# Moving the head sums, the attention product and the weight splits in a fused attention and mixture-of-experts kernel

## The chip, the cores and the metric

One core of one Trainium2 chip runs the kernel. The metric is the device time of one execution in microseconds, as the median of several runs.

## The reference

With `x` of 1 x 1024 x 256 (float32) and `xn` its layernorm, the output is `x + attention(xn) + ffn(xn)`:

```python
qkv = xn @ w_qkv                                  # 256 x 768; 16 heads of 16
q, k = elu(q) + 1, elu(k) + 1
decay = sigmoid(decay_param)                      # one per head
s_t  = decay * s_{t-1} + k_t * v_t                # running_kv
z_t  = decay * z_{t-1} + k_t                      # running_ksum
den  = clip(sum_over_head(q * z), 1e-6)
attention = (q * s / den) @ w_out

e    = argmax(xn @ router_w.T)                    # 8 experts, top 1
gate = sigmoid(top logit)
routed = (silu(g) * u) @ w_down[e],  g, u = split((xn * gate) @ w_gate_up[e])
shared = (silu(g) * u) @ shared_down, g, u = split(xn @ shared_gate_up)
ffn  = routed + shared                            # inner width 512
```

## The kernel before

Every engine has its own hand-written stream; semaphores tie them together. Most products are of split operands: a value is copied to a rounded `_hi` (float32r), the remainder `_lo` is value minus `_hi`, and each product is three matmuls (hi·hi, hi·lo, lo·hi), in `three` (L287) and `qkv_tile` (L898). Tokens are handled in two halves of 512 (four blocks of 128 each).

**Front.** SyncE loads x in four pieces, the k, v and q columns of w_qkv, the shared weights `sgu`, zeros for `sorted_rows`, `sdn`, `wout`, and `gu`/`dn` of experts 0 and 1 (L303 to L320). GpSimd writes constants, then the remainder of q's weights (L407) and of the second half of `sgu` (L412). VectorE does the statistics (`statistics` L606, `variances` L612, `normalise` L620), two normalised blocks of each half, `x_lo` (L632), the weight remainders `w_lo` of k and v (L638), the decay sum (L702), the hi and lo of `sgu`'s first half (L705 to L707), and copies router rows (L713). ScalarE does the square roots, the other two blocks (`norm` L447), the hi parts (`x_hi` L452, L464 to L473, L482) and the Exp of the decay (L477). TensorE warms up (L996), transposes the tokens (L856), then runs twelve `qkv_tile`s (L898) with the router products (`router_logits` L869), the decay product (L1012), `transpose_logits` (L882), `ranks` (L891) and the two products of shared tile 0 in between (L1003 to L1024).

**Middle.** From the logits VectorE chooses the expert (`choose` L645) and places each token in expert-sorted slots of 144 (`place` L657); `plan` holds the end tile of each expert, and every engine reads those ends into registers (`read_end`). ScalarE scales the tokens by the gate (L489) and GpSimd scatters them to `sorted_rows` in DRAM (L421). TensorE runs shared tiles 1 to 6 (`shared_tile` L943), ScalarE their Silu (L528) and `hT_hi` (L517), VectorE the product (`hidden`, L772), the scans of k (`k_scan` L735), q times ksum (`q_ksum` L752) and `hT_lo` (L760).

**Expert loop.** On each engine a loop over tiles runs once for each expert; with these inputs there are eight tiles (t = 0 to 7), one for each expert. TensorE (L1042 to L1072) does in tile t: gate and up products of half h = 0, `transpose_back` of tile t-1's result (L985), products of h = 1, `transpose_sorted` of the rows of tile t+1 (L976), and the down product (L1068). ScalarE does Silu twice, the copy to `xgT` and the copy to `yT` (L548). VectorE multiplies twice into `hr` (L801) and copies the finished rows (`rows_copy` L789), for which the store before must have landed; GpSimd stores them (L429). Between the tiles of certain experts stand pieces of the attention: `kv_scan` (L744), the split of q·ksum (`qk_high` L557, `qk_low` L806), the sums over a head (`denominators` L965, in PSUM bank 7, each followed by `den_copy` L562), the way of `den` through DRAM (L574, L577), clip and reciprocal (L827), the 1 MB write `rden_rows` that repeats each reciprocal for its 16 columns (L580), and its reading back into `rspread` (L359).

SyncE's queue works in order. `rows_of(e)` (L327) issues for each tile t of expert e, once TensorE has transposed tile t+1's rows, the load of the rows of tile t+2; `refill(e)` (L334) adds the loads of `gu` and `dn` for expert e+2, once the products of expert e have been done:

```python
for e in range(E - 2):
    refill(e)
rows_of(6)
sp.wait_ge(s_rdram, 16)          # rden_rows has landed
for c in range(KC):
    sp.dma_start(rspread[...], rden_rows[...]).then_inc(s_spread, 16)
rows_of(7)
```

**Tail.** TensorE does shared tile 7, the last `transpose_back`, then `shared_down` (L1076) and `attention_out` (L1082) for eight token blocks. VectorE copies the last rows, does `hidden(7)`, the remainder of `wout`, the product with `rspread` (L838) and `att_lo` (L842). GpSimd stores the last rows, waits for all stores and gathers the routed result of each block (L438); VectorE adds it and the PSUM result to x (L846, L849), and SyncE stores.

## Time and profile before

| | |
|---|---|
| median of 3 runs (lowest to highest) | 138.3 us (137.26 to 140.29) |
| the profiled execution | 138.7 us |
| its span, first to last instruction | 136.8 us |
| TensorE busy | 125.7 us, 92% |
| VectorE busy | 79.2 us, 58% |
| ScalarE busy | 54.2 us, 40% |
| GpSimd busy | 34.3 us, 25% |
| TensorE's granted clock, mean | 0.992 |

The span is what the rows count from: a start of 54.5 is 54.5 us behind the first instruction. The profiled execution's own time is 1.9 us more than its span. PE is TensorE's matmuls, DVE VectorE, ACT ScalarE, POOL GpSimd, SP SyncE; a q behind the name (SPq, ACTq) is the engine's sequencer, which issues DMAs.

### The profile page before, as it was taken

The page shows a single profiled execution, that of the slowest core. Times are in us where ns is not written, and L with a number is a line of the kernel's source. Part 1 is how long each engine was busy: PE and PEld are TensorE (multiplying, and loading weights), DVE is VectorE, ACT ScalarE, POOL GpSimd, SP SyncE. Part 2 cuts the span into 40 slices and gives each one's busy share as a digit, 9 for nine tenths or more (in the row PEclk, how much of TensorE's full clock was granted, in tenths as well). Part 3 has the DMA queues.
Part 4 walks back from the last instruction along what each step waited for, and adds up shares of the span by engine and source line. Part 5 has one row for each costly group of instructions (what it writes and reads, how often), then busy time and mean ns, then how long its engine had stood idle before and what let it go on. Part 6 is the DMA issues. An engine that isn't in the chain of part 4 may idle for free.

```text
span 136.8 us, 2550 instructions
## 1 busy us (share of the span) xinstructions
PE 125.7 (92%) x830; PEld 108.0 (79%) x830; DVE 79.2 (58%) x159; ACT 54.2 (40%) x106; POOL 34.3 (25%) x57
## 2 busy tenths in 40 slices
PE   4978879999999998999999999999999999999930
PEld 1244446788888885999889899999999989999920
DVE  0787895894338999993635538374040405952663
ACT  4263888449696836325262222313132221600000
POOL 7603043023876000020202010201020011197830
...
GB/s 95 221 223 119 342 334 213 189 397 400 378 133 77 54 5 29 14 62 296 239 350 155 297 261 184 386 222 316 230 292 349 86 256 141 46 6 109 167 233 103
DMA packets 20052, 27.40 MB, mean 200 GB/s; under 512 B 1336, under 2 KB 16864, under 8 KB 20040
## 3 DMA queue, kind: packets, MB, share of 16 engines
...
## 4 chain that ended last, share of the span: by engine, by line
PE 46%; DMA 27%; DVE 9%; issue 7%; POOL 6%; SPq 1%; DVEq 1%; ACT 1%; POOLq 0%
DMA sorted_rows<-yrow 15%; PE ps L1052 13%; PE ps L1068 7%; POOL q_sb L438 6%; DMA sgu<-_ffn_shared_gate_up_dram 4%; PE ps L291 4%; PE ps L290 4%; PE ps L289 4%; DMA wqkv<-in_L_attn_w_qkv_dram 3%; PE ps L918 3%; PE ps L924 3%; PE ps L931 3%; DMA q_sb<-sorted_rows,slot_row 3%; DMA x_sb<-in_L_attn_x_dram 2%; DVE yrow L793 2%
## 5 line engine op out<-in xcount | busy, mean ns | idle before, releaser
L1052 PE MATMUL ps<-xgT,gu 128*128 128x144 f32 x256 | 34.1, 286 | 0.7 <-DVE sgu L772 0.7
L1052 PEld LDWEIGHTS ps<-xgT,gu 128*128 128x128 f32 x256 | 32.5, 190 | 1.4 <-ACT xgT L513 1.1
L429 POOL DMA_DIRECT2D sorted_rows<-yrow x8 | 5.6, 699 | 61.1 <-DVE yrow L793 61.1
L801 DVE TENSOR_TENSOR wqkv<-rz,ps 128x288 f32<-128x288 f32 x16 | 7.2, 452 | 23.4 <-ACT rz L552 23.4
L1068 PE MATMUL ps<-wqkv,dn 128*128 128x144 f32 x128 | 17.8, 291 | 0.1
L1068 PEld LDWEIGHTS ps<-wqkv,dn 128*128 128x128 f32 x128 | 16.2, 190 | 0.5 <-DVE wqkv L801 0.3
L552 ACT ACTIVATE rz<-ps 128x288 f32<-128x288 f32 x16 | 6.6, 410 | 23.5 <-PE ps L1052 23.5
L289 PE MATMUL ps<-xT_hi,sgu_hi 128*128 128x512 f32 x32 | 12.8, 399 | 0.0
L291 PE MATMUL ps<-xT_hi,sgu_lo 128*128 128x512 f32 x32 | 12.5, 390 | 0.0
L290 PE MATMUL ps<-xT_lo,sgu_hi 128*128 128x512 f32 x32 | 12.5, 389 | 0.0
L438 POOL DMA_INDIRECT q_sb<-sorted_rows,slot_row x8 | 9.9, 1243 | 4.9 <-POOLq L434 2.7
L793 DVE COPY yrow<-ps 72x512 f32<-72x512 f32 x9 | 6.1, 683 | 8.6 <-DMA sorted_rows<-yrow 8.5
L421 POOL DMA_INDIRECT sorted_rows<-xn,slot_row x8 | 8.7, 1083 | 5.5 <-ACT xn L489 3.7
L918 PE MATMUL ps<-xT_hi,wqkv_hi 128*128 128x512 f32 x24 | 8.2, 420 | 1.2 <-ACT xT_hi L455 0.8
L290 PE MATMUL ps<-wqkv_lo,hT_hi 128*128 128x256 f32 x32 | 9.0, 283 | 0.0
L289 PE MATMUL ps<-wqkv_hi,hT_hi 128*128 128x256 f32 x32 | 9.0, 282 | 0.0
L517 ACT ACTIVATE hT_hi<-sgu 128x512 fp32r<-128x512 f32 x8 | 5.1, 632 | 10.0 <-DVE sgu L772 10.0
L291 PE MATMUL ps<-wqkv_hi,hT_lo 128*128 128x256 f32 x32 | 9.0, 281 | 0.0
L555 ACT ACTIVATE yT<-ps 128x288 f32<-128x288 f32 x8 | 3.3, 412 | 13.0 <-PE ps L1068 13.0
L931 PE MATMUL ps<-xT_hi,wqkv_lo 128*128 128x512 f32 x24 | 7.7, 400 | 0.2 <-DVE wqkv_lo L640 0.2
L924 PE MATMUL ps<-xT_lo,wqkv_hi 128*128 128x512 f32 x24 | 7.6, 396 | 0.0
L996 PE MATMUL ps<-ones 128*128 128x512 bf16 x14 | 5.6, 511 | 1.8 <-POOL ones L373 1.8
...
## 6 DMA issues: line engine op xcount, KB each, us to landing
...
rden_rows<-rden ACTq DMA_DIRECT2D x1, 1024.0 KB, 11.2
```

The lines of the kernel that those rows point to most:

```text
L289: nc.tensor.matmul(o, w_hi, m_hi, start=start, stop=False)
L290: nc.tensor.matmul(o, w_hi, m_lo, start=False, stop=False)
L291: return nc.tensor.matmul(o, w_lo, m_hi, start=False, stop=stop)
L421: pool.indirect_dma_start(sorted_rows, bass.IndirectOffsetOnAxis(ap=slot_row[:, i:i + 1], axis=0), xn[:, i, :], None).then_inc(s_scatter, 16)
L438: pool.indirect_dma_start(y_tok[:, i, :], None, sorted_rows, bass.IndirectOffsetOnAxis(ap=slot_row[:, i:i + 1], axis=0)).then_inc(s_gather ...
L793: V.tensor_copy(yrow[:, :, :].rearrange("p j d -> p (j d)"), ps[0:HS, 7, :]).then_inc(s_yrow, 1)
L801: V.tensor_tensor(hr[:, 2 * h:2 * h + 2, :].rearrange("p f s -> p (f s)"), act_sb[:, h, 0:2 * SLOTS], ps[:, 2 * h + 1, 0:2 * SLOTS], ALU.m ...
L918: mm(o, wqkv_hi[:, kc, cols], xT_hi[:, kc, rows], start=(kc == 0), stop=False)
L924: ins = mm(o, wqkv_hi[:, kc, cols], xT_lo[:, kc, rows], start=False, stop=last and kc == KC - 1)
L931: ins = mm(o, wqkv_lo[:, kc, cols], xT_hi[:, kc, rows], start=False, stop=last and kc == KC - 1)
L1052: ins = mm(ps[:, 2 * h + u, (f % 2) * SLOTS:(f % 2 + 1) * SLOTS], gu[p][:, kc, col:col + P], xgT[:, kc, :], start=(kc == 0), stop=(kc == K ...
L1068: ins = mm(ps[:, 5 + c, 0:SLOTS], dn[p][:, f, c * P:(c + 1) * P], hr[:, f, :], start=(f == 0), stop=(f == FC - 1))
```

## The change

- q's weight remainder is computed by VectorE behind v's, not by GpSimd. The v columns are loaded ahead of the second half of x, and ScalarE splits v ahead of q.
- The shared weights: ScalarE makes both hi halves (behind the second products of qkv tiles 2 and 5), VectorE both remainders behind the third q, and nothing of it stands on GpSimd or ahead of `x_lo(1)`. Shared tile 0 comes behind all twelve qkv tiles.
- VectorE normalises three of the first half's blocks, ScalarE one; ScalarE's `norm(1)` comes ahead of the decay's Exp; VectorE copies the router rows ahead of `x_lo(1)`; the first `router_logits` comes ahead of the second `transpose_tokens`; the decay product comes behind `ranks`.
- Both head sums stand behind expert 1 (banks 7 and 4) and the den chain follows from there: load behind expert 2's tiles, reciprocal and the write `rden_rows` behind expert 3's. SyncE waits for that write and reads it back between `refill(3)` and `refill(4)`.
- The product q·kvsum moves from behind expert 3 to behind expert 4, the product with `rspread`, `att_hi` and `att_lo` come ahead of the last rows.

```diff
@@ -282,6 +280,7 @@
         gate_bank = [4, 0, 2, 4, 0, 2, 4, 2]
+        den_bank = [7, 4]
@@ -304,9 +303,9 @@
             sp.wait_ge(s_x[1], 16)
+            w_load(2, s_wv)
...
             x_load(3)
-            w_load(2, s_wv)
@@ -350,15 +349,16 @@
             sp.dma_start(xg, sorted_rows[2 * SLOTS:3 * SLOTS, :].rearrange("(j p) d -> p j d", p=HS)).then_inc(s_xg, 16)
-            for e in range(E - 2):
+            for e in range(4):
                 refill(e)
-            rows_of(6)
...
             sp.wait_ge(s_rdram, 16)
...
                              rden_rows.rearrange("(i c p) t -> c p i t", c=KC, p=P)[c]).then_inc(s_spread, 16)
-            rows_of(7)
+            for e in range(4, E - 2):
+                refill(e)
+            for e in range(E - 2, E):
+                rows_of(e)
@@ -403,14 +403,6 @@
-            pool.wait_ge(s_whq, 1)
-            pool.tensor_tensor(wqkv_lo[:, :, 0:D], wqkv[:, :, 0:D], wqkv_hi[:, :, 0:D].bitcast(F32), ALU.subtract).then_inc(s_wlq, 1)
...
-            for h in range(2):
-                pool.wait_ge(s_shi, h + 1)
-                cols = slice(h * F, (h + 1) * F)
-                pool.tensor_tensor(sgu_lo[:, 1, cols], sgu[:, 1, cols], sgu_hi[:, 1, cols].bitcast(F32), ALU.subtract).then_inc(s_slo, 1)
@@ -446,7 +438,7 @@
                 act.wait_ge(s_rstd, n + 1)
-                for i in (n * TH + 2, n * TH + 3):
+                for i in range(n * TH + (3, 2)[n], (n + 1) * TH):
@@ -467,19 +459,16 @@
             x_hi(0)
+            act.wait_ge(s_wv, 16)
+            A(wqkv_hi[:, :, 2 * D:3 * D], wqkv[:, :, 2 * D:3 * D], ACT.Copy).then_inc(s_whv, 1)
...
             A(wqkv_hi[:, :, 0:D], wqkv[:, :, 0:D], ACT.Copy).then_inc(s_whq, 1)
-            act.wait_ge(s_wv, 16)
-            A(wqkv_hi[:, :, 2 * D:3 * D], wqkv[:, :, 2 * D:3 * D], ACT.Copy).then_inc(s_whv, 1)
...
             A(sd[:, TH:NT], mv[:, TH:NT, 1], ACT.Sqrt, bias=eps[:, 0:1]).then_inc(s_sd, 1)
+            norm(1)
...
             A(dec_e[:, :], dec_in[:, :], ACT.Exp, scale=-1.0).then_inc(s_dece, 1)
-            norm(1)
             x_hi(1)
-            act.wait_ge(s_sgu, 16)
-            for h in range(2):
-                A(sgu_hi[:, 1, h * F:(h + 1) * F], sgu[:, 1, h * F:(h + 1) * F], ACT.Copy).then_inc(s_shi, 1)
@@ -502,6 +491,10 @@
                         A(lrow[:, 1, :], ps[0:2 * E, ROUTE, :], ACT.Copy).then_inc(s_lcopy, 1)
+                    if t in (2, 5):
+                        c = t // 3
+                        act.wait_ge(s_sgu, 16)
+                        A(sgu_hi[:, c, :], sgu[:, c, :], ACT.Copy).then_inc(s_shi, 1)
@@ -531,7 +524,7 @@
                 if k < 6:
-                    read_end((0, 1, 2, 3, 5, 7)[k])
+                    read_end((0, 1, 2, 3, 6, 7)[k])
@@ -543,7 +536,7 @@
             hidden_hi(LAST - 1)
-            one_, two, three_, four, six, total = ends
+            one_, two, three_, four, seven, total = ends
@@ -561,29 +554,29 @@
                 act.wait_ge(s_den, n + 1)
-                A(den_h[:, n * 512:(n + 1) * 512], ps[0:HEADS, 7, :], ACT.Copy).then_inc(s_denc, 1)
+                A(den_h[:, n * 512:(n + 1) * 512], ps[0:HEADS, den_bank[n], :], ACT.Copy).then_inc(s_denc, 1)
...
             qk_high(0)
+            qk_high(1)
...
             den_copy(0)
-            qk_high(1)
-            expert_tiles(two, three_)
...
             act.dma_start(den_rows.rearrange("(i h) t -> h i t", h=HEADS), den_h.rearrange("h (i t) -> h i t", t=P)).then_inc(s_denst, 16)
-            expert_tiles(three_, four)
+            expert_tiles(two, three_)
...
             act.dma_start(den[:, :], den_rows).then_inc(s_denld, 16)
-            expert_tiles(four, six)
+            expert_tiles(three_, four)
...
             act.dma_start(rden_rows.rearrange("(q d) t -> q d t", d=HD), rden[:, :].unsqueeze(1).broadcast_to([NT * HEADS, HD, P])).then_inc(s_rdram, 16)
-            expert_tiles(six, total)
-            gate_silu(LAST)
-            hidden_hi(LAST)
+            expert_tiles(four, seven)
...
                 A(att_hi[:, c, :], kvsum[:, c, :], ACT.Copy).then_inc(s_atth, 1)
+            expert_tiles(seven, total)
+            gate_silu(LAST)
+            hidden_hi(LAST)
@@ -626,7 +619,7 @@
                 V.scalar_tensor_tensor(shift[:, h], mv[:, h, 0], -1.0, rstd[:, h], ALU.mult, ALU.mult).then_inc(s_rstd, 1)
-                for i in (n * TH, n * TH + 1):
+                for i in range(n * TH, n * TH + (3, 2)[n]):
@@ -649,7 +642,7 @@
                 link(V.tensor_tensor(is_top[:, :, :], logits[:, :, :], top[:, :].unsqueeze(1).broadcast_to([P, E, NT]), ALU.is_equal))
-                dve.wait_ge(s_const, 19)
+                dve.wait_ge(s_const, 20)
@@ -693,6 +686,8 @@
             w_lo(2).then_inc(s_wlv, 1)
+            dve.wait_ge(s_whq, 1)
+            w_lo(0).then_inc(s_wlq, 1)
@@ -701,16 +696,12 @@
             V.reciprocal(dec_h[:, :], dec_1[:, :]).then_inc(s_dech, 1)
-            dve.wait_ge(s_sgu, 16)
-            V.tensor_copy(sgu_hi[:, 0, :], sgu[:, 0, :]).then_inc(s_sgh, 1)
-            dve.wait_ge(s_sgh, 1)
-            V.tensor_tensor(sgu_lo[:, 0, :], sgu[:, 0, :], sgu_hi[:, 0, :].bitcast(F32), ALU.subtract).then_inc(s_sgl, 1)
-            x_lo(1)
...
             V.tensor_copy(lrow[:, 0, :], ps[0:2 * E, ROUTE, :]).then_inc(s_lcopy, 1)
+            x_lo(1)
@@ -722,15 +713,18 @@
                 V.tensor_tensor(kvsum[:, c, cols], ksum[:, c, cols], ps[:, (3 * a + 1) % 4, :], ALU.mult).then_inc(s_kv, 1)
-                if a == 0:
-                    dve.wait_ge(s_decp, 1)
-                    V.tensor_copy(decay[:, :], ps[:, 7, 64:64 + KC]).then_inc(s_decay, 1)
...
                     place()
+                if a == KC:
+                    for h in range(KC):
+                        dve.wait_ge(s_shi, h + 1)
+                        V.tensor_tensor(sgu_lo[:, h, :], sgu[:, h, :], sgu_hi[:, h, :].bitcast(F32), ALU.subtract).then_inc(s_slo, 1)
+                    dve.wait_ge(s_decp, 1)
+                    V.tensor_copy(decay[:, :], ps[:, 7, 256:256 + KC]).then_inc(s_decay, 1)
@@ -771,12 +765,11 @@
-            dve.wait_ge(s_sgl, 1)
+            dve.wait_ge(s_slo, KC)
...
                 hidden(k)
-                if k < 6:
-                    read_end((0, 1, 2, 3, 4, 7)[k])
+                read_end((0, 1, 2, 3, 4, 6, 7)[k])
@@ -792,7 +785,7 @@
-            one_, two, three_, four, five, total = ends
+            one_, two, three_, four, five, seven, total = ends
@@ -814,32 +807,33 @@
             qk_low(0)
+            qk_low(1)
+            expert_tiles(two, three_)
             kv_scan(2)
-            expert_tiles(two, three_)
-            qk_low(1)
...
             expert_tiles(three_, four)
-            for c in range(KC):
-                dve.wait_ge(s_kvs, 2 * NH)
-                V.tensor_tensor(kvsum[:, c, :], q_sb[:, c, :], kvsum[:, c, :], ALU.mult).then_inc(s_qkv_sum, 1)
-            expert_tiles(four, five)
...
             V.tensor_tensor(sdn_lo, sdn[:, :, :], sdn_hi.bitcast(F32), ALU.subtract).then_inc(s_plo, 1)
-            expert_tiles(five, total)
-            rows_copy(total)
-            hidden(LAST)
+            expert_tiles(four, five)
+            for c in range(KC):
+                dve.wait_ge(s_kvs, 2 * NH)
+                V.tensor_tensor(kvsum[:, c, :], q_sb[:, c, :], kvsum[:, c, :], ALU.mult).then_inc(s_qkv_sum, 1)
             V.tensor_tensor(wout_lo, wout[:, :, :], wout_hi.bitcast(F32), ALU.subtract).then_inc(s_plo, 1)
+            expert_tiles(five, seven)
...
                 V.tensor_tensor(kvsum[:, c, :], kvsum[:, c, :], rspread[:, c, :], ALU.mult).then_inc(s_att, 1)
-            hidden_lo(LAST)
+            expert_tiles(seven, total)
...
                 V.tensor_tensor(att_lo[:, c, :], kvsum[:, c, :], att_hi[:, c, :].bitcast(F32), ALU.subtract).then_inc(s_attl, 1)
+            rows_copy(total)
+            hidden(LAST)
+            hidden_lo(LAST)
@@ -854,12 +848,12 @@
             def transpose_tokens(n):
-                for j in range(TH):
+                for j in ((0, 3, 1, 2), (0, 1, 2, 3))[n]:
                     i = n * TH + j
-                    if j < 2:
-                        pe.wait_ge(s_xn, 2 * n + j + 1)
+                    if j < (3, 2)[n]:
+                        pe.wait_ge(s_xn, 3 * n + j + 1)
                     else:
-                        pe.wait_ge(s_xna, 2 * n + j - 1)
+                        pe.wait_ge(s_xna, (1, j)[n])
@@ -881,7 +875,6 @@
-                pe.wait_ge(s_decay, 1)
@@ -951,10 +944,7 @@
                     if k == 0:
-                        if kc == 0:
-                            pe.wait_ge(s_sgl, 1)
-                        else:
-                            pe.wait_ge(s_slo, u + 1)
+                        pe.wait_ge(s_slo, kc + 1)
@@ -965,9 +955,9 @@
                 cols = slice(n * 512, (n + 1) * 512)
-                pe.wait_ge(s_yrow, end + 1)
+                pe.wait_ge((s_yrow, s_xgc)[n], end + 1)
                 pe.wait_ge(s_qkl, KC * (n + 1))
-                o = ps[0:HEADS, 7, :]
+                o = ps[0:HEADS, den_bank[n], :]
@@ -1002,25 +992,21 @@
                 qkv_tile(t)
+            router_logits(0)
             transpose_tokens(1)
-            router_logits(0)
...
-            pe.wait_ge(s_dech, 1)
-            for c in range(KC):
-                ins = mm(ps[:, 7, 64 + c:65 + c], spread[:, c, :], dec_h[:, :], start=True, stop=True)
-            ins.then_inc(s_decp, 1)
...
             ranks()
-            for t in range(7, 10):
-                qkv_tile(t)
-            for u in range(2):
-                shared_tile(0, u)
-            for t in range(10, 12):
+            pe.wait_ge(s_dech, 1)
+            for c in range(KC):
+                ins = mm(ps[:, 7, 256 + c:257 + c], spread[:, c, :], dec_h[:, :], start=True, stop=True)
+            ins.then_inc(s_decp, 1)
+            for t in range(7, 12):
@@ -1030,7 +1016,7 @@
             pe.wait_ge(s_plan, 1)
-            for k in range(1, LAST):
+            for k in range(LAST):
@@ -1054,8 +1040,8 @@
                             pe.wait_ge(s_yrow, t + 1)
-                            if e in (2, 3):
-                                pe.wait_ge(s_denc, e - 1)
+                            if e == 2:
+                                pe.wait_ge(s_denc, NH)
@@ -1068,8 +1054,9 @@
                     ins.then_inc(s_down, 1)
-                if e in (1, 2):
-                    denominators(e - 1, ends[e])
+                if e == 1:
+                    for n in range(NH):
+                        denominators(n, ends[e])
```

## Rows read from the trace of the kernel before

**Rows 1.** The page, parts 1 (busy us, share, instructions) and 4 (chain, by line)
```profile
PE 125.7 (92%) x830; PEld 108.0 (79%) x830; DVE 79.2 (58%) x159; ACT 54.2 (40%) x106; POOL 34.3 (25%) x57
...
DMA sorted_rows<-yrow 15%; PE ps L1052 13%; PE ps L1068 7%; POOL q_sb L438 6%; DMA sgu<-_ffn_shared_gate_up_dram 4%; PE ps L291 4%; PE ps L290 4%; PE ps L289 4%; DMA wqkv<-in_L_attn_w_qkv_dram 3%; PE ps L918 3%; PE ps L924 3%; PE ps L931 3%; DMA q_sb<-sorted_rows,slot_row 3%; DMA x_sb<-in_L_attn_x_dram 2%; DVE yrow L793 2%
```

**Rows 2.** Chain that ended last, front: start us, us, what
```profile
10.46 6.07 DMA sgu<-_ffn_shared_gate_up_dram
...
20.44 0.40 PE ps L877
```

**Rows 3.** Timeline of VectorE and GpSimd, front: start, us, instruction, idle before
```profile
7.61 0.68 DVE L640 TENSOR_TENSOR wqkv_lo<-wqkv,wqkv_hi 128x512 fp32r<-128x512 f32 x1
...
11.65 1.35 DVE L640 TENSOR_TENSOR wqkv_lo<-wqkv,wqkv_hi 128x512 fp32r<-128x512 f32 x1 [0.93 <-ACT wqkv_hi L473]
...
12.93 0.74 DVE L610 BATCH_NORM_STATS2 bn<-x_sb 128x6 f32<-128x256 f32 x2
...
15.33 0.73 DVE L630 TENSOR_SCALAR xn<-x_sb,mv,rstd 128x256 f32<-128x256 f32 x2
...
11.18 1.27 POOL L407 TENSOR_TENSOR wqkv_lo<-wqkv,wqkv_hi 128x512 fp32r<-128x512 f32 x1 [5.48 <-ACT wqkv_hi L471]
```

**Rows 4.** Timeline of ScalarE, front
```profile
14.43 1.28 ACT L477 ACT_TABLE_LOAD   x1
...
15.83 1.08 ACT L450 ACTIVATE xn<-x_sb,shift,rstd 128x256 f32<-128x256 f32 x2
```

**Rows 5.** Timeline of TensorE and VectorE, expert loop
```profile
54.51 2.22 PE L1052 MATMUL ps<-xgT,gu 128*128 128x144 f32 x16 [0.65 <-DVE sgu L772]
...
94.71 0.41 PE L982 MATMUL ps<-ident,wqkv 72*128 72x72 f32 x4
...
96.97 2.12 PE L1052 MATMUL ps<-xgT,gu 128*128 128x144 f32 x16
...
67.02 1.28 DVE L810 TENSOR_TENSOR att_lo<-ksum,att_hi 128x512 fp32r<-128x512 f32 x2
```

**Rows 6.** Issues (SyncE, ScalarE), landing of rspread and rden_rows, of den, and windows
```profile
82.70 0.37 SPq L340 DMA_DIRECT2D gu<-in_L_ffn_w_gate_up_dram  x1
...
88.71 0.37 SPq L325 DMA_DIRECT2D wqkv<-sorted_rows  x1
...
95.94 0.38 SPq L340 DMA_DIRECT2D gu<-in_L_ffn_w_gate_up_dram  x1
...
84.07 0.36 ACTq L577 DMA_DIRECT2D den<-den_rows  x1
...
97.31 0.60 ACTq L580 DMA_DIRECT2D rden_rows<-rden  x1
...
DMA to landing us min/median/max: 3.9/4.9/11.2
...
den<-den_rows ACTq DMA_DIRECT2D x1, 64.0 KB, 5.3
...
97.30:108.50 11.20, 11.20 (x97) 11.18 (x96) 2.25 (x5) 2.58 (x8) 0.69 (x1) 1.00 0.85 266
...
112.00:113.00 1.00, 1.00 (x8) 0.86 (x7) 0.00 (x0) 0.58 (x1) 0.00 (x0) 1.00 1.15 348
```

**Rows 7.** Timeline of the tail, GpSimd, VectorE, TensorE
```profile
119.30 3.10 POOL L438 DMA_INDIRECT q_sb<-sorted_rows,slot_row  x1 [2.75 <-POOLq L434]
...
126.05 0.42 DVE L849 TENSOR_TENSOR x_sb<-x_sb,ps 128x256 f32<-128x256 f32 x1 [1.43 <-PE ps L291]
...
134.24 0.42 DVE L849 TENSOR_TENSOR x_sb<-x_sb,ps 128x256 f32<-128x256 f32 x1
...
130.77 0.28 PE L291 MATMUL ps<-wqkv_hi,att_lo 128*128 128x256 f32 x1
```

**Rows 8.** Windows: stretch, us, five engines' busy time, granted clock, DMA share, GB/s
```profile
134.00:135.00 1.00, 0.00 (x0) 0.00 (x0) 0.56 (x2) 0.00 (x0) 0.00 (x0) 0.82 0.32 113
...
135.00:136.00 1.00, 0.00 (x0) 0.00 (x0) 0.00 (x0) 0.00 (x0) 0.00 (x0) 0.50 0.44 152
```

6 lines of the change are left out of this document (2 added, 4 removed).

## The prediction

> **What bounds the kernel now.** I read the page first: TensorE is busy for 125.7 of 136.8 us and most lines of the chain that ended last are its own [rows 1]. So an idle time of any other engine matters only where TensorE waits for it, and I went along TensorE's timeline looking for its waits. Three stretches came out.
>
> The front, up to 20.4 us. The second half's remainder xT_lo stands on VectorE behind sgu_hi and sgu_lo of the shared weights, and those behind their load, which landed at 16.5; TensorE restarts with the router product at 20.44 [rows 2]. From there it doesn't stop until 54.51, where it waits 0.65 us for the sixth hidden product [rows 5].
>
> The expert loop, 54.5 to 110.3. There are eight tiles here, one for each expert, 6.6 us each, and the weight and row loads arrive in time: tile 6 starts at 96.97, the moment tile 5's down product ends [rows 5].
>
> The tail. The chain goes through the stores of yrow (15% of the span) and the eight gathers of GpSimd at L438 (6%) [rows 1], not through TensorE: its last matmul starts at 130.77, the last add at 134.24 [rows 7]. The profiled execution is 138.7 us for a span of 136.8, 0.4 above the median of 138.3; I sum against 138.7 and take 0.4 off at the end.
>
> **The front.** Removed: GpSimd's subtraction for q (1.27 us) and both for the shared weights, VectorE's sgu_hi and sgu_lo ahead of xT_lo. Added on VectorE: q's subtraction behind v's. V's took 1.35 us against 0.68 for k's; beside it ran GpSimd's own, 11.18 to 12.45 [rows 3]. 12.45 plus 0.6 is 13.0, where v's ended: VectorE stood until GpSimd was through. Without GpSimd there, v's and q's cost 0.68 each, 1.36 together, so this edit alone is free for VectorE, and what remains as its gain is the order (v's weights loaded and split first, so that TensorE's second tile and its 0.38 us wait go). If 1.35 were instead the price of the instruction itself, the front would gain 1.3 less.
>
> The Trainium skill has this as a rule ("SBUF — State Buffer", section "Who interferes with whom"): VectorE with two SBUF inputs and a GpSimd instruction that reads SBUF share a port, and the one that issues second waits for the whole of the other. By that rule 0.68 stands, and the trace agrees (0.68 alone, 1.35 beside GpSimd); by the opposite reading the total below would be 1.3 us more.
>
> After the change v's weights come to ScalarE by about 9.6 and q's as now, so VectorE has q's remainder at 11.9 and the statistics of the last two blocks start there, 1.0 us before the 12.93 of now. From there to the first block that is normalised with the new rstd it is 2.4 us (15.33) [rows 3], so 14.3; then ScalarE: two blocks of norm 1.09, and now the table load for Exp, which stood ahead of norm under VectorE's work (14.43 to 15.7), comes behind it: 1.28 and 0.20 [rows 4], making 16.9. x_hi starts there, not at 17.44. VectorE meanwhile waits for that Exp (two small instructions, 0.3), copies lrow (0.6) and does xT_lo, 1.3: 19.2. The router product starts at 19.3 instead of 20.44, 1.1 gained. The decay products only move. ScalarE's two sgu_hi and VectorE's two sgu_lo (some 1.1 and 1.2 each, twice a 128x512) lie beside qkv tiles: sgu_lo is done near 33.1, TensorE reaches the shared tiles at 33.0 and their second half at 33.7. GpSimd's scatter may stand behind a sgu_lo for up to 1.2 us a time; its rows aren't needed until 51. The shared tiles then end at 52.6, and the hidden product that TensorE waited 0.65 us for comes at 51.4 since ScalarE and VectorE start theirs 2.9 us sooner. Sum of the front: 1.1 + 0.65, with rounding **-1.8** (bounds -0.7 and -2.6).
>
> **The head sums.** They cost 0.92 twice now and 0.92 twice then. VectorE comes to its first remainders at 67.02, two in 1.28, so four end near 69.5; the second sum could begin at 69.37 (68.45 and one sum) [rows 5]: **+0.15** (0 to 0.5). ScalarE's second pair of qk_hi, 1.1 us more behind tile 0, makes a Silu 0.6 late, and the down product that needs it comes 2 us later. kv_scan 2 and 3, 2.5 us, take the place behind tile 2 that a pair of remainders and one scan have now, 2.5 us too.
>
> **The wait on SyncE, the term that decides.** The den load is issued one tile earlier, at 76.3 in today's times, and takes 5.3 us [rows 6]: 81.7, before VectorE is through with tile 3 (82.56). The clip and reciprocal, 1.2, end at 83.8, so ScalarE issues the write rden_rows at 84.07, where it has its slot behind tile 3 and where today's den load is issued. It is the 1,024 KB write that today is issued at 97.31 and lands 11.2 us later. In both places it follows a gu load (with dn behind it) by the same 1.37 us: 95.94 now, 82.70 then [rows 6]. So I take the same 11.2 us, to 95.3. Bounds: 4.9 us, in which the rspread pair, the same megabyte read back alone, landed; and 12.5, if the loads beside it weigh more [rows 6].
>
> SyncE's queue is in order, and in the changed code it waits for that write between refill(3) and refill(4). It reaches the wait at 84.3. Behind it stand: both rspread loads; the load of tile 6's rows, now issued at 88.71; gu for expert 6, right after it; its dn [rows 6]. Who waits for these: TensorE, at 94.71, for tile 6's rows (the transposes inside tile 5) and at 96.97 for gu [rows 5]. Today SyncE does the same wait behind its last refill, with nothing behind it that is late.
>
> With the release at 95.3, the rspread issues take 1.0, and tile 6's rows are issued at 96.6, behind 1 MB of the same queue. Rspread landed at most 4.9 us after its issue [rows 6]; 144 KB more at the 348 GB/s of that read are 0.4: rows at 95.3 + 5.3 = 100.6. gu is 1 MB more, 3.0: 103.6. Tile 6 then starts at 103.6 and not 96.97: 6.6 us if TensorE resumes at full speed.
>
> It has then stood for 5.7 us. At the end of the profile the granted clock goes from 1.00 to 0.50 (2.4 to 1.2 GHz) near 134.6, 3.7 us after the last matmul [rows 8]. So I take it to be at 1.2 GHz at 100.6: four transposes and the down product, 2.25 us, take 4.5, to 105.1, and the gu wait lies under that. The term is 105.1 - 96.97 = **+8.1**. Its bounds: 0 if the write lands within 5.3 us (by 89.4), 6.6 with the clock kept, 10.1 if the next half tile is slow too. Later loads catch up: gu and dn of expert 7 are issued near 102 and used from 111 on. The earlier tiles' stores, which also pass through the congestion, lie under the stall.
>
> The clock is also the subject of the page "TensorE: Matmul & The Clock Gate", section "Part 1: The HAM clock gate", of the Trainium skill: an idle TensorE is put back to half its clock, and only sustained work restores it. By that rule 1.5 us or more of the 8.1 come from the clock; were it kept, the total would be 1.5 lower. The fall in the profile's last microseconds agrees; no row here has dense matmuls right after a fall.
>
> **The tail.** The attention product, att_hi and att_lo now stand ahead of the last rows_copy: 2.35 us of VectorE work before tile 7 and 2.35 behind its last product, and 2.2 on ScalarE. Ahead of a tile's first product VectorE idles for longer than that, and the last att_lo ends before the transposed rows come: free. Were it not, 1 us. The stores no longer meet the rden write and rspread, so rows_copy, store and gathers start some 2 us earlier against the loop's end, and the first gather, 3.10 beside att_lo against 0.95 for the others [rows 7], falls to 0.95. Then TensorE is the later: 20.6 us of shared down and out products behind the loop, as now. The adds follow its tiles, from 126.05, and a pair of 0.42 us adds takes 0.86 with the gap [rows 7]: the last ends at 132.5 against 134.66. **-2.2** (0 to -2.5).
>
> **The sum.** 138.7 - 1.8 + 0.15 + 8.1 - 2.2 = 142.95 for a profiled execution; less 0.4 as a median: **142.5 us**.
>
> **The rivals.**
> No stall: the write lands by 89.4, or its wait is hidden. For it: the same write would have less store and row traffic beside it. Against: 11.2 us in the same phase, with the DMA engines 0.85 busy through it [rows 6]. Time: 142.5 - 8.1 = 134.4, 2.8% faster. This is the case on the other side; it decides from a landing under 5.3 us after the issue. Chance 0.13.
> Half a stall: the write takes 8 us, or rows slip in between rspread's packets; 2 to 5 us are lost: 136.4 to 139.4. Chance 0.12.
> Full stall, clock kept: 142.5 - 1.5 = 141.0, right at 2%. Chance 0.17.
> Full stall and slow restart, my forecast: chance 0.5. The last 0.08: the same, with the front's gain missing (VectorE's table wait, scatter) or a longer slow clock, 143.5 to 145.
>
> **From these to the numbers.** A measurement tells about 2% from no change: under 135.5 is faster, over 141.1 slower. Faster: 0.14 with a strong front. Slower: 0.5, 0.08 and a little under half of the clock-kept case, less something for a smaller stall: 0.6. The rest, 0.26, is within. The range leaves out the case without a stall: 137.5 to 144.8; the likeliest case's own is 141.3 to 144.5.
>
> **What would show it.** Right: SyncE's wait for rden_rows near 11 us, the tile 6 rows issued after it; one TensorE wait of about 6 us in the sixth tile for the load of wqkv, with a granted clock at 0.5 behind it; the router product near 19.3; the expert loop from 52.7; the first gather under 1.3 us. Wrong: a write that lands in 5 us, TensorE without a gap between 85 and 105, a time under 136.

## The result and the profile after

The changed kernel took 145.18 us as the median of 4 runs (143.43 to 148.63), the kernel before 138.49 (137.26 to 140.29, 4 runs) beside it: a ratio of 1.0472, 95% interval 1.0325 to 1.0619. Forecast were 142.5 us and a range of 137.5 to 144.8. So the sign is right, and the time lies 0.4 us above the range. Executions more than 1.5% above the fastest of their kernel are left out of every ratio here; medians and ranges are over all of them. The profiled execution took 145.27 us for a span of 143.3.

The page of the changed kernel, parts 1 and 4, against [rows 1]:

```profile
PE 127.4 (89%) x830; PEld 110.9 (77%) x830; DVE 79.8 (56%) x161; ACT 53.9 (38%) x105; POOL 28.5 (20%) x54
...
PE 71%; DMA 15%; DVE 7%; ACT 2%; issue 1%; SPq 1%; POOL 0%; DVEq 0%; ACTq 0%; POOLq 0%
PE ps L1038 14%; PE ps L1054 10%; PE ps L288 9%; PE ps L289 9%; PE ps L290 9%; DMA rden_rows<-rden 7%; DMA den<-den_rows 4%; PE ps L986 4%; DMA wqkv<-sorted_rows 3%; PE ps L911 3%; PE ps L924 3%; PE ps L917 3%; PE ps L980 2%; DVE xT_lo L629 2%; PE ps L972 2%
```

Before, the chain of waits ran through the stores and GpSimd's gathers. Now the gathers are gone from it, and three transfers stand there that weren't on it: the read of den (4%), the write rden_rows (7%) and the rows of one tile (3%). They are 14% of 143.3 us, in the middle of the expert loop. TensorE's records alone add 1.7 us of busy time for the same count of matmuls: some ran slower.

The front, timelines of VectorE and TensorE (start, us, instruction, idle before), against [rows 2, 3]:

```profile
10.99 1.28 DVE L633 TENSOR_TENSOR wqkv_lo<-wqkv,wqkv_hi 128x512 fp32r<-128x512 f32 x2
...
12.20 0.74 DVE L603 BATCH_NORM_STATS2 bn<-x_sb 128x6 f32<-128x256 f32 x2
...
19.70 0.39 PE L871 MATMUL ps<-xT_hi,rT 128*16 128x512 f32 x1 [1.99 <-DVE xT_lo L629]
...
53.09 2.14 PE L1038 MATMUL ps<-xgT,gu 128*128 128x144 f32 x16
```

The two remainders take 1.28 together where one of them took 1.35 beside GpSimd's. The router product comes at 19.70 and not at 20.44, though TensorE now stands 1.99 us ahead of it, and the expert loop starts at 53.09 and not at 54.51 [rows 5].

The issues that matter in the middle (SyncE and ScalarE), against [rows 6], and what SyncE waited for between 75 and 105 us:

```profile
83.10 0.60 ACTq L572 DMA_DIRECT2D rden_rows<-rden  x1
...
93.37 1.00 SPq L356 DMA_DIRECT2D ksum<-rden_rows  x2
95.98 0.39 SPq L324 DMA_DIRECT2D wqkv<-sorted_rows  x1
96.64 0.38 SPq L339 DMA_DIRECT2D gu<-in_L_ffn_w_gate_up_dram  x1
```

```profile
SPq L356 <- DMA rden_rows<-rden: 10.9, 1, 10.9
```

TensorE meanwhile, tiles 5 to 7:

```profile
88.53 2.12 PE L1038 MATMUL ps<-xgT,gu 128*128 128x144 f32 x16
...
90.92 2.13 PE L1038 MATMUL ps<-xgT,gu 128*128 128x144 f32 x16
100.63 0.74 PE L972 MATMUL ps<-ident,wqkv 72*128 72x72 f32 x4 [7.58 <-DMA wqkv<-sorted_rows]
101.16 4.14 PE L1054 MATMUL ps<-wqkv,dn 128*128 128x144 f32 x16
105.09 2.83 PE L1038 MATMUL ps<-xgT,gu 128*128 128x144 f32 x16
...
112.42 2.12 PE L1038 MATMUL ps<-xgT,gu 128*128 128x144 f32 x16
```

From tile 5's start to tile 7's it is 23.89 us, and 13.24 for two tiles that wait for nothing (two of 6.62). The loss is 10.65 us: 7.58 of waiting, and some 3 us in which the same 16 matmuls take 4.14 instead of 2.17 and the next ones 2.83 instead of 2.12. The windows show the clock through this stretch (stretch, us, five engines' busy time, granted clock, DMA share, GB/s):

```profile
94.00:95.00 1.00, 0.00 (x0) 0.00 (x0) 0.00 (x0) 0.00 (x0) 0.68 (x1) 1.00 0.16 23
95.00:96.00 1.00, 0.00 (x0) 0.00 (x0) 0.00 (x0) 0.00 (x0) 0.00 (x0) 1.00 0.83 238
96.00:97.00 1.00, 0.00 (x0) 0.00 (x0) 0.00 (x0) 0.00 (x0) 0.00 (x0) 0.64 1.10 329
97.00:106.00 9.00, 5.37 (x24) 5.38 (x25) 0.00 (x0) 0.82 (x2) 0.00 (x0) 0.50 1.04 360
106.00:107.00 1.00, 1.00 (x8) 1.00 (x7) 0.00 (x0) 0.00 (x0) 0.00 (x0) 0.74 0.84 333
```

The granted clock fell from 1.00 to 0.50 (2.4 to 1.2 GHz) near 96.3, with TensorE idle since 93.05, and came back near 106.5, 5.9 us after it resumed. In 94 to 95 hardly a byte moved (23 GB/s): the write had landed, rspread, issued at 93.37, wasn't moving yet, and the rows weren't issued before 95.98.

The tail, timelines of GpSimd and VectorE, against [rows 7]:

```profile
125.98 1.04 POOL L430 DMA_INDIRECT q_sb<-sorted_rows,slot_row  x1 [2.73 <-POOLq L426]
```

```profile
134.68 0.42 DVE L843 TENSOR_TENSOR x_sb<-x_sb,ps 128x256 f32<-128x256 f32 x1 [5.50 <-PE ps L290]
...
140.70 0.42 DVE L843 TENSOR_TENSOR x_sb<-x_sb,ps 128x256 f32<-128x256 f32 x1
```

The first gather takes 1.04 instead of 3.10. Before, att_lo's two subtractions ran on VectorE from 119.13 to 121.48 and the gather beside them until 122.40; now att_lo is over at 120.14, before the gather starts. From TensorE's product on, the adds wait only for TensorE, and from the loop's end (118.94) to the last add's end it is 22.18 us instead of 24.35.

Together: -1.82 up to tile 5, +10.65, -0.2 in tile 7 (6.52 us and not 6.72), -2.17 is +6.46 us. The spans differ by 6.5 us and the two profiled executions by 145.27 - 138.7 = 6.57.

### The profile page after: what moved, and what is told of

It reads as the page before. It is cut to its first block, busy times and chain, and to the rows that moved or that the text cites. A ratio compares the mean times of both kernels' runs of the same rounds, so it can differ in the third digit from the quotient of the medians.

```text
span 143.3 us, 2550 instructions
## 1 busy us (share of the span) xinstructions
PE 127.4 (89%) x830; PEld 110.9 (77%) x830; DVE 79.8 (56%) x161; ACT 53.9 (38%) x105; POOL 28.5 (20%) x54
## 4 chain that ended last, share of the span: by engine, by line
PE 71%; DMA 15%; DVE 7%; ACT 2%; issue 1%; SPq 1%; POOL 0%; DVEq 0%; ACTq 0%; POOLq 0%
PE ps L1038 14%; PE ps L1054 10%; PE ps L288 9%; PE ps L289 9%; PE ps L290 9%; DMA rden_rows<-rden 7%; DMA den<-den_rows 4%; PE ps L986 4%; DMA wqkv<-sorted_rows 3%; PE ps L911 3%; PE ps L924 3%; PE ps L917 3%; PE ps L980 2%; DVE xT_lo L629 2%; PE ps L972 2%
## 5 line engine op out<-in xcount | busy, mean ns | idle before, releaser
L1038 PE MATMUL ps<-xgT,gu 128*128 128x144 f32 x256 | 34.7, 290 | 0.0
L1038 PEld LDWEIGHTS ps<-xgT,gu 128*128 128x128 f32 x256 | 33.2, 194 | 0.4 <-ACT xgT L506 0.2
L1054 PE MATMUL ps<-wqkv,dn 128*128 128x144 f32 x128 | 19.4, 310 | 0.0
L1054 PEld LDWEIGHTS ps<-wqkv,dn 128*128 128x128 f32 x128 | 18.0, 208 | 0.0
L972 PE MATMUL ps<-ident,wqkv 72*128 72x72 f32 x36 | 4.1, 238 | 7.6 <-DMA wqkv<-sorted_rows 7.6
L972 PEld LDWEIGHTS ps<-ident,wqkv 72*128 72x128 f32 x36 | 3.7, 149 | 7.9 <-DMA wqkv<-sorted_rows 7.8
L430 POOL DMA_INDIRECT q_sb<-sorted_rows,slot_row x8 | 7.8, 969 | 4.9 <-POOLq L426 2.7
L548 ACT ACTIVATE yT<-ps 128x288 f32<-128x288 f32 x8 | 3.3, 410 | 14.4 <-PE ps L1054 14.4
## 6 DMA issues: line engine op xcount, KB each, us to landing
rden_rows<-rden ACTq DMA_DIRECT2D x1, 1024.0 KB, 10.3
```

Source lines behind the costliest of these rows:

```text
L430: pool.indirect_dma_start(y_tok[:, i, :], None, sorted_rows, bass.IndirectOffsetOnAxis(ap=slot_row[:, i:i + 1], axis=0)).then_inc(s_gather ...
L972: ins = tr(ps[:, bank, col:col + HS], xg[:, j, c * P:(c + 1) * P], ident[0:HS, 0:HS])
L1038: ins = mm(ps[:, 2 * h + u, (f % 2) * SLOTS:(f % 2 + 1) * SLOTS], gu[p][:, kc, col:col + P], xgT[:, kc, :], start=(kc == 0), stop=(kc == K ...
L1054: ins = mm(ps[:, 5 + c, 0:SLOTS], dn[p][:, f, c * P:(c + 1) * P], hr[:, f, :], start=(f == 0), stop=(f == FC - 1))
```

## The experiments

The difference between kernels is taken inside one session on one chip; the kernel before was run in each (138.62 for e1 to e4, 138.97 for e5 to e8, 141.13 for e9 to e12, 141.05 for e13 and e14). These are four sessions on three chips: e9 to e14 ran on one chip.

**e1: the wait and rspread behind the last refill but two.** The write stays as early as the change has it; only SyncE's place for the wait moves.

```diff
-            for e in range(4):
+            for e in range(E - 2):
                 refill(e)
             sp.wait_ge(s_rdram, 16)
...
-            for e in range(4, E - 2):
-                refill(e)
```

> The changed kernel with one edit: SyncE waits for rden_rows and issues both rspread loads behind refill(5), not between refill(3) and refill(4). Theory A (the wait on SyncE's queue with what it does to the clock is the whole loss of the loop, 10.6 us): no wait of TensorE for the load of wqkv in the expert loop, granted clock 1.00 until the tail, time 145.2 - 10.6 = 134.6 us, ratio to before 0.97. Rival B (the DMA engines are too full for the rden write, whoever waits for it: expert weights and rows are late anyway): waits of several us remain in tiles 5 and 6, time over 139 us.

Measured: 141.55 us (138.06 to 144.92, 10 runs), ratio 1.0072 (1.0011 to 1.0133). The 7.6 us wait is gone, yet the gain is far from whole. VectorE and TensorE of this run:

```profile
108.77 2.36 DVE L827 TENSOR_TENSOR kvsum<-kvsum,ksum 128x1024 f32<-128x1024 f32 x2 [4.54 <-DMA ksum<-rden_rows]
```

```profile
113.06 3.76 PE L1052 MATMUL ps<-wqkv,dn 128*128 128x144 f32 x16 [2.91 <-DVE wqkv L792]
```

The write now runs beside tile 6's and 7's loads and takes 14.4 us, rspread is issued at 100.57, and the attention product, which the change has put ahead of tile 7's products on VectorE, waits 4.54 us for it; TensorE's down product waits 2.91 behind that, and the granted clock falls to 0.50 there, so that the product takes 3.76 us and not 2.17. So the order of the queue was one cause and the early due time of the product is a second, which the first had covered (e5 tests this). This execution lost 2.6 us in the front as well (below).

**e2: the wait behind one refill more than in the change.**

```diff
-            for e in range(4):
+            for e in range(E - 3):
                 refill(e)
...
-            for e in range(4, E - 2):
-                refill(e)
+            refill(E - 3)
```

> As the run before, with the wait and the rspread loads between refill(4) and refill(5). The write lands at about 93.4 us and refill(4) ends at 88.5. Theory A (only what stands behind the wait when the write lands is late): rows of tile 6 and gu of expert 6 are in time; the rows of tile 7 are due near 93.7, behind 1 MB of rspread, and gu of expert 7 near 94.5, both needed only at 100 and 102: 0 to 1 us lost, 134.6 to 135.6 us. Rival B (a full DMA queue): 139 us or more, as much as the changed kernel has.

Measured: 140.92 us (139.69 to 144.55, 4 runs; too spread for a ratio). The write took 12.4 us, and now tile 7's rows are behind it. Tile 6's rows and gu come late too, by 0.69 and 0.24 us. TensorE, and a window of the same kernel:

```profile
103.02 0.47 PE L971 MATMUL ps<-ident,wqkv 72*128 72x72 f32 x4 [1.91 <-DMA wqkv<-sorted_rows]
```

```profile
103.00:108.00 5.00, 4.98 (x29) 4.99 (x30) 1.86 (x2) 1.82 (x4) 0.00 (x0) 0.66 0.67 248
```

Behind this wait of 1.91 us the clock fell: a mean of 0.66 over the next 5 us costs 1.7 us (down product 3.23, the next ones 2.78), nearly as much as the wait. With the product due ahead of tile 7, none of the three places tried for the wait (the change, e2, e1) is free.

**e3: the wait where the change has it, tile 6's rows and weights ahead of rspread.**

```diff
             sp.wait_ge(s_rdram, 16)
+            refill(4)
             for c in range(KC):
...
-            for e in range(4, E - 2):
-                refill(e)
+            refill(5)
```

> The changed kernel with the wait for rden_rows where it is, but refill(4) ahead of the two rspread loads. It parts the stall in the wait for the write and the megabyte read ahead of the rows. Theory A: the rows of tile 6 are issued at 93.8 and land near 97, 3.6 us less stall; gu of expert 6 is issued at 94.4 and lands 6.8 us later at 101.2, where tile 6 could start at 99.2, so TensorE has two waits, about 4 and 2 us, and the clock may hold through both: total loss about 6 us in place of 10.6, 140.6 us. If the clock falls all the same: 142 to 143. Rival B (the rows wait for the write alone, rspread costs nothing): no change against 145.2.

Measured: 145.09 us (143.55 to 146.59, 4 runs), ratio 1.0515 (1.0421 to 1.0608). SyncE and TensorE:

```profile
96.01 0.37 SPq L324 DMA_DIRECT2D wqkv<-sorted_rows  x1
```

```profile
98.66 0.74 PE L972 MATMUL ps<-ident,wqkv 72*128 72x72 f32 x4 [4.39 <-DMA wqkv<-sorted_rows]
```

The rows land 2.65 us after their issue, against 4.65 behind rspread, and TensorE's wait falls from 7.58 to 4.39; the clock falls here too (down product 4.14). Tile 5's start to tile 7's is 21.01 us, 2.9 less than in the changed kernel. 1.2 of it went in the front, where the clock fell in this execution and not in the changed kernel's, so the profiled executions are 1.7 us apart; the medians (145.09 and 145.18) don't show it. What the run settles is the gap ahead of the rows: the write was issued at 84.01 and landed 10.4 later, at 94.4, and the rows went at 96.01, 1.6 us later with nothing of rspread between. In the changed kernel it is 1.6 too, from the end of rspread's issues (94.37) to 95.98. It is 1.6 in e1, e4, e9 and e12 as well, and 1.1 in e2. By the code, SyncE has there to read the loop's bound from the plan and to enter the loop; the profile doesn't show these instructions, so that they take the time is inferred.

**e4: TensorE kept busy in the wait.** 28 matmuls of ones, whose result nobody reads, stand ahead of tile 5's transposes.

```diff
+                    if e == 5:
+                        for _ in range(28):
+                            mm(ps[:, 4, :], ones[:, :], ones[:, :].unsqueeze(1).broadcast_to([P, 4, P]), start=True, stop=True)
                     transpose_sorted(4, s_xg, 16 * t + 16)
```

> The changed kernel with 28 matmuls of ones (512 columns each, some 6.1 us, result unused) ahead of the transposes in tile 5, in the time in which TensorE waits for the rows of tile 6. Theory A (3 us of the 10.6 are the clock, which fell while TensorE stood still): the wait ends at the same time, the clock stays at 1.00, the down product takes 2.17 and not 4.14 us, but gu of expert 6 may then be waited for 0.5 to 1 us: 142.3 to 143.1 us. Rival C (the slow down product comes from the loads that run beside it, not from the standstill): down product still near 4 us, time 145.2 or more.

Measured: 143.05 us (142.68 to 144.19, 4 runs), ratio 1.0342 (1.025 to 1.0435), 2.1 below the changed kernel and e3. TensorE:

```profile
94.03 6.21 PE L1050 MATMUL ps<-ones 128*128 128x512 bf16 x28
101.35 0.47 PE L972 MATMUL ps<-ident,wqkv 72*128 72x72 f32 x4 [1.11 <-DMA wqkv<-sorted_rows]
101.65 2.17 PE L1057 MATMUL ps<-wqkv,dn 128*128 128x144 f32 x16
103.81 2.22 PE L1038 MATMUL ps<-xgT,gu 128*128 128x144 f32 x16
```

The rows come no sooner (7.36 us behind the release, where the change has 7.26), but the down product takes 2.17 again and the next ones 2.22. The rival, that the loads beside it slow the product, is out: they are there (DMA share 1.03 over the product) and it isn't slow. The slow clock is 2 to 3 us of the loss, by this run and by the trace of the change.

**e5: e1, and the attention product with att_hi and att_lo behind tile 7.**

```diff
             expert_tiles(five, seven)
+            expert_tiles(seven, total)
             dve.wait_ge(s_spread, 16 * KC)
...
-            expert_tiles(seven, total)
+            rows_copy(total)
+            hidden(LAST)
             for c in range(KC):
                 dve.wait_ge(s_atth, c + 1)
```

> e1 (rspread loads behind refill(5)) with the product with rspread, att_hi and att_lo behind tile 7 and not ahead of it. In e1 the write took 14.4 us beside the refills, rspread landed at 108.4 or later, VectorE stood in front of tile 7's products and TensorE waited 2.9 us for hr. Theory D (what is left of the loss in e1 is the place of the attention product, which makes the end of the den chain due before tile 7): TensorE's 2.9 us wait goes, time 135.4 us where e1's fast runs have 138.1 to 139.9. Rival E (the product ahead of the last rows was worth its 2.2 us in the tail, and putting it back gives as much back as it takes): 137.5 to 138.5 us, no change.

Measured: 137.75 us (135.58 to 138.76, 6 runs), ratio 0.9854 (0.9765 to 0.9943): the first version whose interval lies below the kernel before, if by less than 2%. In its profile the 2.91 us for which TensorE waited in e1 are gone. Its executions sort by their mean granted clock: 135.58 and 136.12 at 1.00, 137.52 and 137.97 at 0.985 to 0.987, 138.69 and 138.76 at 0.975. The profiled one is of the last kind (windows):

```profile
19.00:24.00 5.00, 4.45 (x19) 3.03 (x20) 2.47 (x5) 4.03 (x7) 0.00 (x0) 0.69 1.10 249
24.00:28.00 4.00, 4.00 (x11) 3.10 (x12) 2.66 (x8) 1.25 (x3) 0.69 (x1) 0.54 1.11 289
```

11 matmul records in 24 to 28 where the changed kernel's trace has 21: the clock falls right behind the router product (near 20.9), that is behind the 1.99 us for which TensorE stands ahead of it. The loop then starts at 55.78, 2.7 later than 53.09. So at full clock the kernel gives what was expected of it (135.4), and the front takes part of it back.

**e6: the kernel before with the front of the change alone** (loads, remainders, norm and Exp in the change's order, the shared weights split on ScalarE and VectorE as in the change; head sums, attention product and SyncE's wait as before).

```diff
+            w_load(2, s_wv)
             x_load(2)
             x_load(3)
-            w_load(2, s_wv)
...
             w_lo(2).then_inc(s_wlv, 1)
+            dve.wait_ge(s_whq, 1)
+            w_lo(0).then_inc(s_wlq, 1)
...
+            norm(1)
             act.wait_ge(s_dec, 16)
             A(dec_e[:, :], dec_in[:, :], ACT.Exp, scale=-1.0).then_inc(s_dece, 1)
-            norm(1)
             x_hi(1)
```

> The kernel before with the front of the change alone: v ahead of q, q's remainder on VectorE, the splits of the shared weights, shared tile 0 and the decay product behind the qkv tiles, three and one blocks of norm; expert loop, den chain, SyncE's order and tail as before. If the front is worth what the trace of the changed kernel shows (expert loop from 53.1 in place of 54.5): 138.6 - 1.4 = 137.2 us. Rival F (TensorE now stands 2.0 us in one piece ahead of the second router product, and in some executions the granted clock falls there, as in e1's profiled run, where the qkv tiles behind it took 0.85 us a pair and not 0.47): a mean clock under 0.98 in a part of the executions, these at 139 to 140, and a median that is no better than before.

Measured: 137.49 us (136.52 to 138.27, 4 runs), ratio 0.9929 (0.9857 to 1.0001). So the front is worth about 1.5 us of 138.97, as expected, with an interval that just reaches no change. The clock fell in the profiled execution here too (0.66 over 19 to 24 us, loop start 54.25). The rival had executions with a mean clock under 0.98 at 139 to 140 us, and none of the four is one.

**e7: e5, with q's remainder back on GpSimd.** This undoes one move of the change's front, in the kernel without the stall.

```diff
+            pool.wait_ge(s_whq, 1)
+            pool.tensor_tensor(wqkv_lo[:, :, 0:D], wqkv[:, :, 0:D], wqkv_hi[:, :, 0:D].bitcast(F32), ALU.subtract).then_inc(s_wlq, 1)
...
-            dve.wait_ge(s_whq, 1)
-            w_lo(0).then_inc(s_wlq, 1)
```

> e5 with the remainder of q's weights back on GpSimd. Theory G (GpSimd and VectorE exclude each other only for the length of one instruction, and VectorE is the engine that sets the front): VectorE's subtraction for v starts first and takes 0.68, GpSimd's follows until about 12.9, a microsecond before TensorE wants it; VectorE has 0.6 us less to do ahead of the statistics, so the router product starts 0.6 earlier, and the time falls by 0.6 us against e5. Rival H (GpSimd gets in first and VectorE's 0.68 becomes 1.35 as in the kernel before, or the statistics stand behind it too): no change or up to 0.7 us more.

Measured: 135.43 us (134.03 to 135.93, 6 runs), ratio 0.9769 (0.9707 to 0.9831), 2.3 below e5, and all six at 0.995 or more of full clock. VectorE, GpSimd and TensorE in the front:

```profile
10.64 0.68 DVE L633 TENSOR_TENSOR wqkv_lo<-wqkv,wqkv_hi 128x512 fp32r<-128x512 f32 x1
```

```profile
18.74 0.39 PE L869 MATMUL ps<-xT_hi,rT 128*16 128x512 f32 x1 [1.45 <-DVE xT_lo L629]
```

With v's weights loaded first, v's remainder starts 0.55 us ahead of GpSimd's for q (11.19, 1.29 us) and takes 0.68, so neither stands behind the other as in [rows 3]; the statistics, with one input, start at 11.24 and not 12.20, and TensorE stands 1.45 instead of 1.99. The mean of the six is 0.6 us below that of e5's two executions at full clock, the 0.6 expected, though the six spread over 1.9 us. The rest is a clock that fell in four of e5's six executions and in none of these.

**e8: e5, with the decay's Exp behind x_hi(1).**

```diff
+            x_hi(1)
             act.wait_ge(s_dec, 16)
             A(dec_e[:, :], dec_in[:, :], ACT.Exp, scale=-1.0).then_inc(s_dece, 1)
-            x_hi(1)
```

> e5 with the Exp of the decay, and so its table load of 1.28 us, behind x_hi(1) on ScalarE, and the decay sum on VectorE behind xT_lo. Theory F (it is this table load that lets TensorE stand 2.0 us ahead of the second router product, and that standstill lets the clock fall in some executions): the router product starts near 18.1 and not 19.7; qkv tile 4 still waits for the first k, whose Exp comes at the same time as now, so the wait is split in two of 0.5 and 1.2 us and only 0.4 us are gained, but fewer executions have a mean clock under 0.99: median 135.0 us. Rival I: the falls come as often, since the busy share of the stretch is the same.

Measured: 136.12 us (135.58 to 138.63, 6 runs), ratio 0.9822 (0.9769 to 0.9874). TensorE:

```profile
20.60 0.71 PE L909 MATMUL ps<-xT_hi,wqkv_hi 128*128 128x512 f32 x2 [1.51 <-DVE ksum L710]
```

The router product comes at 18.01 (18.1 expected), but the next qkv tile only at 20.60, where the changed kernel has 20.62: it waits 1.51 us for VectorE's key sum, which waits for the Exp of k. The 0.4 us expected don't come (the loop starts at 53.09, as in the changed kernel); what the run gains on e5 is again a clock that seldom falls: four of six executions are at 0.995 or more of full clock.

**e9: the changed kernel with q's remainder on GpSimd**, by the same edit as e7. **e12: the changed kernel again**, beside it.

> The changed kernel with q's remainder back on GpSimd, nothing else. Theory G (this one edit costs VectorE 0.6 us in front of the statistics, and through the longer standstill of TensorE it brings falls of the clock in some executions): router product at 18.8 in place of 19.7, no slow qkv tiles, the stall in the loop as it was: 144.2 us against 145.2 in the same session, and no execution near 148. Rival J (the stall in the loop absorbs it, since the rden write is issued with the loop and the loads beside it are the same): everything is 0.9 earlier, so the full 0.9 must show unless the write itself then takes longer: 145 us.

> The changed kernel once more, on the same chip and beside the same runs of before as e9 to e11, for their comparison: 145.2 us, ratio 1.047, clocks 0.94 to 0.975.

Measured, e9 and e12 in turn: 148.48 us (147.74 to 149.37, 4 runs), ratio 1.0564 (1.0496 to 1.0631), and 149.03 (148.01 to 151.63, 5 runs), ratio 1.0551 (1.0494 to 1.0608). TensorE waits 7.92 us for tile 6's rows in e9 and 7.05 in e12. So q's engine makes 0.5 us in the changed kernel, where 1.0 was expected; these runs don't resolve either from nothing, and the loss is there with both engines.

**e10: e7 and e8 together.**

> e7 (q's remainder on GpSimd, rspread behind refill(5), product behind tile 7) with e8's Exp of the decay behind x_hi(1). Theory F and G together: k's first Exp comes 0.6 earlier than in e8 since norm(1) does, qkv tile 4 starts at 20.0 or before, 0.3 us earlier than in e7: 135.1 us against e7's 135.4. Rival: e7's tile 4 already starts with the first k's Exp, so nothing is gained: 135.4 to 135.7.

Measured: 141.26 us (140.12 to 143.75, 12 runs), ratio 0.9999 (0.996 to 1.0038). Tile 4 of qkv stands where e8's does:

```profile
20.54 0.70 PE L909 MATMUL ps<-xT_hi,wqkv_hi 128*128 128x512 f32 x2 [1.50 <-DVE ksum L710]
```

The two edits don't add up, and together they are worse than e7's alone: e7's kernel starts this tile at 19.66, and on this chip (e13) at 19.65, 0.9 earlier. e10's expert loop starts at 54.37 and e13's at 52.66, and the medians are 1.7 us apart in the same sense, with the kernel before at 141.13 and 141.05 beside them. So the later Exp costs e7's kernel time in the front. The rest of the 1.7 isn't traced.

**e11: e5, with 8 matmuls of ones ahead of the second router product.**

```diff
             qkv_tile(3)
+            for _ in range(8):
+                mm(ps[:, 7, :], ones[:, :], ones[:, :].unsqueeze(1).broadcast_to([P, 4, P]), start=True, stop=True)
             router_logits(1)
```

> e5 with eight matmuls of ones (512 columns, 1.8 us, result unused) ahead of the second router product, in the 2.2 us in which TensorE stands there. Theory F (this standstill is what makes the clock fall behind it in half of the executions): mean clock 0.99 or more in all executions and none over 137; median 136.0 us, the fast end of e5 (135.6 to 136.1), in place of 137.75. Rival K (the falls come from something else in the front, the lower use of TensorE in its first 20 us or the chip's own state): the same spread as e5, 135.6 to 138.8, with clocks down to 0.975.

Measured: 140.25 us (139.36 to 142.07, 12 runs), ratio 0.9954 (0.9915 to 0.9994), all twelve at 0.987 or more, eight of them at the 0.99 expected or above. e5's kernel on the same chip is e14: 140.40 us, ratio 0.9962, five of twelve under 0.987. So the filler goes with fewer low clocks, and the median gains nothing that these runs resolve.

**e13: e7 again. e14: e5 again**, both on the chip of e9 to e12.

> The same kernel as e7, beside e5's kernel (the next run) on one chip. If q's remainder on GpSimd is what keeps TensorE's standstill ahead of the router product short and its clock up, this one is 1 to 2 us below the other on any chip, few or none of its executions have a granted clock under 0.99, and it is 2% below the kernel before: ratio 0.975 to 0.985. If e7's 0.9769 was an effect of that chip or session (on another chip the kernel with GpSimd and the moved Exp gave 0.9999), the ratio is 0.99 or more, and the gap to the other within 0.6 us.

> e5's kernel again: q's remainder on VectorE. If the clock falls in its front in about half of its executions, as in e5, its median lies 1 to 2 us above e13's and its executions split by clock (those at 1.00 near e13 plus 0.6, those at 0.975 to 0.985 some 2 us more). If not, it is 0.6 us above e13, the difference of the two fronts at full clock.

Measured: e13 139.59 us (median of 11), ratio 0.9923 (0.9881 to 0.9966); e14 140.40 (median of 12), ratio 0.9962 (0.9922 to 1.0001). One of e14's executions took 706.67 us, as one of the kernel before's took 706.63; nothing on record says why, and neither is in a ratio. The order of the two kernels holds, 0.8 us apart, but their intervals overlap, as e7's and e5's do; five of e14's twelve have a mean clock under 0.987 and none of e13's but one, which is at 0.851. The size doesn't hold: 0.8% here, 2.3% in e7. TensorE of e13:

```profile
94.25 0.47 PE L970 MATMUL ps<-ident,wqkv 72*128 72x72 f32 x4 [1.18 <-DMA wqkv<-sorted_rows]
...
97.01 2.22 PE L1036 MATMUL ps<-xgT,gu 128*128 128x144 f32 x16 [0.29 <-DMA gu<-in_L_ffn_w_gate_up_dram]
...
108.91 0.47 PE L970 MATMUL ps<-ident,wqkv 72*128 72x72 f32 x4 [0.54 <-DMA wqkv<-sorted_rows]
```

In e7's trace TensorE has none of these three waits (2.0 us together): there the write took 7.8 us and here 14.4. Of the eight traces with an early write and the wait behind refill(5), six show such waits for rows or gu in tiles 4 to 7 (e1, e5, e8, e10, e11, e13: 0.24 to 2.0 us in all), and the kernel before and e6, which write at 97.3 and 96.8, show none. That the early write takes bandwidth from loads that are nearly due fits this, but no run tests it alone. e7's kernel lies below the kernel before in both sessions, by 2.3 and 0.8%, the second within 2%; it lies far below the changed one.

## Why the prediction was right or wrong

**The front, -1.8 and the head sums, +0.15: the number right, partly by luck.** Statistics came at 12.20 (forecast 11.9) and the router product at 19.70 (19.3), so it gained 0.74 and not 1.1, and the loop starts 1.42 earlier and not 1.8. Tile 4 starts 1.82 earlier all the same (81.91 and not 83.73; the forecast was 1.65). The head sums cost a gap of 0.27 (67.47 to 67.74) for the forecast's 0.15, and a wait in tile 1 went that the forecast didn't have. In the kernel before VectorE copied the finished rows late, having waited for their store, and TensorE's down product had to stop for its second half:

```profile
66.05 0.69 DVE L793 COPY yrow<-ps 72x512 f32<-72x512 f32 x1 [1.77 <-DMA sorted_rows<-yrow]
```

```profile
65.84 2.56 PE L1068 MATMUL ps<-wqkv,dn 128*128 128x144 f32 x16
```

In the changed kernel this copy waits for nothing and the product takes 2.17. The choice of 0.68 a remainder held: 1.28 for two, alone. What no step had is that the longer standstill ahead of the router product lets the clock fall in some executions; in the nine traces with this front and no filler (the change, e1 to e6, e12, e14) it did in six, for 1.2 or about 2.7 us. The profiled execution of the change had none of it, so the sum isn't touched, but e1, e5 and e6 are.

**The wait on SyncE, +8.1: the mechanism right, the term 2.55 us too small. This is the step that failed, and nearly the whole miss (2.3 us by the profiled executions, 2.7 by the medians).** The chain is the forecast's step by step: den in 6.2 (5.3), write issued at 83.10, landed 10.3 later (11.2), rspread released at 93.37; in the times of the changed kernel the forecast was 93.5. That this fits so well is luck: the write started 0.85 later than forecast and landed 0.9 faster. From there it went wrong. Rows landed 7.26 us behind the release and not 5.3 (7.36, 7.31 and 7.0 in e4, e9 and e12): 1.0 for the rspread issues as forecast; 1.6 until the next issue, where the sum had 0.3 without a row for it; and 4.65 to land, where it had 4.0. e3 shows that the 1.6 stands there without rspread too, and that rspread ahead costs the rows 2 us of landing. Then the clock: the transposes and the down product took 4.46 us at 1.2 GHz, as forecast (4.5), but the sum let the clock return with them, and 0.7 more were lost in tile 6. 1.3 + 0.65 + 0.7 are 2.65, less 0.1 for a release that came 0.1 before the forecast's. The last part differs by execution: tile 6 loses 0.0 in e9, 0.3 in e12 and 0.9 in e3. The bound of 10.1, "if the next half tile is slow too", had the last part.

**The tail, -2.2: right** (-2.17), and for the stated reasons: first gather 1.04, TensorE the later one, adds at 0.86 a pair. In all sixteen traces the first gather takes 3.1 us in the two where att_lo's subtractions run beside it (the kernel before, e6) and 1.04 or 1.05 in the others. VectorE's last copy of rows, which waited 5.19 us for a store before, now waits 1.01 for TensorE.

**The rivals.** No stall (134.4) wasn't reached by the change, and e1 and e2 show that the place of the wait alone wouldn't have reached it either (141.55, 140.92). Within 1 to 2 us of it came the kernels with the product moved as well (e5: 135.58 and 136.12 at full clock) and with the shorter standstill (e7: 135.43). The rival was priced as if the write's landing alone decided; three due times did: tile 6's rows, the product ahead of tile 7, and loads beside the write. The rival with the clock kept (141.0) is e4, at 143.05, its distance from the changed kernel being the 2.1 us that the forecast had as 1.5. The Trainium skill's page "TensorE: Matmul & The Clock Gate", section "Part 1: The HAM clock gate", has an idle TensorE put back to half its clock and sustained work restoring it; the trace agrees, with 5.9 us from TensorE's restart, all at 0.50, to the return (3.6 in e9, 5.1 in e12, 6.4 in e3).

**The signs.** Of those named, all came but in size: SyncE's wait 10.9 (near 11), one TensorE wait of 7.6 (about 6), a clock of 0.5 behind it, router product 19.70, loop from 53.09 (52.7), first gather 1.04 (under 1.3).
